# An adaLN block with guided-trajectory attention and two windowed-attention layers: setup as steps, roots by a seed and small operations, unit multiply per tile, padded stream, folded norm, Gelu steps together

## The reference

```python
mod = silu(c) @ wmod                        # sa, ca, ga, sb, cb, gb; ga, gb kept at 0.25 or more in size
h = layernorm(x) * (1 + ca) + sa
x = x + ga * guided_trajectories(h)         # normed steps, dots with 64 guides, softmax, weighted sum
y = layernorm(x) * (1 + cb) + sb
for l in range(2):
    h = shift_token(y)                      # features 64..127 come from the row before, zero in front
    q, k, v = split(h @ wqkv[l])            # 8 heads of 64
    q, k = rotary(l2norm(q) * qs, l2norm(k) * ks)
    y = y + local_attention(q, k, v) @ wo[l]          # windows of 64 rows, each sees the one before
    h = (shift_token(y) - mu) / sqrt(var + 1e-5) * ln_g[l] + ln_b[l]
    a, g = split(h @ w1[l] + b1[l])         # 341 columns each
    y = y + (a * gelu(g)) @ w2[l] + b2[l]
x = x + gb * y
```

## Time and profile before

| what | value |
| --- | --- |
| three runs, median (lowest to highest) | 967.34 us (966.5 to 968.35) |
| the profiled execution | 966.96 us, of which 965.0 is its span |
| mean granted TensorE clock | 0.942 |
| PE / DVE / ACT / POOL busy | 786.4 / 668.0 / 659.3 / 539.6 us |
| ACT's table loads | 40, each 1.283 us |
| power of 128x32 on POOL | 32 times, 5438 ns each |
| DVE's unit multiply 128x2048 | 32 times, 2534 ns each |
| DVE's L1393, bank by rotary table | 128 times, 684 ns each |

### The profile page before, as it was taken

The page is one execution under the profiler, slowest core; times in us unless marked ns, Lnnn a source line. Parts: engine busy times, 40 slices in busy tenths (PEclk is TensorE's granted clock), DMA queues, the critical chain, the costliest instruction groups (busy, mean ns, idle before and its releaser), DMA issues.

```text
span 965.0 us, 19306 instructions
## 1 busy us (share of the span) xinstructions
PE 786.4 (81%) x7151; PEld 556.3 (58%) x7151; DVE 668.0 (69%) x1588; ACT 659.3 (68%) x1545; POOL 539.6 (56%) x324
## 2 busy tenths in 40 slices
PE   4456788879889989888969979888888989888874
PEld 4334566656556666655657656656565666656543
DVE  4566876685687877586887967486787776676732
ACT  0234766867576985877786886877675887868672
POOL 2046853493956653394985643293966690576600
PEclk9668789999899999999999999999999999999997
DMA  6000000000000000000000000000000000000000
GB/s 206 0 12 1 12 2 1 1 1 2 1 2 1 23 2 22 2 1 1 1 1 2 23 1 23 1 2 1 1 1 2 12 2 13 2 1 2 1 1 22
DMA packets 12275, 9.85 MB, mean 10 GB/s; under 512 B 1040, under 2 KB 11288, under 8 KB 12184
## 3 DMA queue, kind: packets, MB, share of 16 engines
q1 hardware_dynamic: 12184, 8.64, 3.0%
HBM read 6.54 MB, written 2.10 MB: 9 GB/s over the span
## 4 chain that ended last, share of the span: by engine, by line
PE 40%; DVE 20%; ACT 19%; issue 11%; POOL 9%; DMA 0%; SPq 0%; POOLq 0%; ACTq 0%; DVEq 0%
ACT probs L964 7%; PE pair L696 6%; PE mixed L727 5%; POOL qk L1494 4%; PE dense L831 4%; PE pair L759 3%; DVE space L1393 3%; DVE q_norm L1398 3%; PE dense L795 3%; PE dense L796 2%; PE dense L797 2%; DVE qk L1195 2%; PE dense L908 2%; ACT squares L1083 2%; ACT probs_t L972 2%
## 5 line engine op out<-in xcount | busy, mean ns | idle before, releaser
L1494 POOL TENSOR_TENSOR qk<-space 128x512 f32<-128x512 f32 x128 | 186.4, 1463 | 58.0 <-DVE q_norm L1398 55.1
L1454 POOL TENSOR_TENSOR root<-power,minus_half 128x32 f32<-128x32 f32 x32 | 174.0, 5438 | 4.6 <-DVE power L1404 4.6
L964 ACT ACTIVATE probs<-pair,neg_max 128x128 f32<-128x128 f32 x512 | 138.3, 402 | 18.9 <-DVE neg_max L1215 18.5
L1393 DVE TENSOR_TENSOR space<-dense,tables 128x512 f32<-128x512 f32 x128 | 87.5, 684 | 36.9 <-ACT space L1087 35.2
L908 PE MATMUL dense<-wq_hi,h_hi 128*128 128x512 f32 x192 | 90.2, 470 | 26.6 <-DVE space L1393 10.9
L1491 POOL TENSOR_TENSOR space<-space,tables 128x512 f32<-128x512 f32 x64 | 82.7, 1293 | 50.7 <-ACT space L1087 50.7
L696 PE MATMUL pair<-eye_s,probs 128*128 128x128 f32 x512 | 80.9, 292 | 34.9 <-ACT probs L964 34.7
L1215 DVE TENSOR_REDUCE neg_max<-pair 128x4 f32<-128x512 f32 x128 | 82.0, 684 | 35.2 <-PE pair L759 35.1
L1083 ACT ACTIVATE squares<-dense 128x512 f32<-128x512 f32 x128 | 79.1, 618 | 39.5 <-PE dense L910 38.6
L696 PEld LDWEIGHTS pair<-eye_s,probs 128*128 128x128 f32 x512 | 59.1, 146 | 56.2 <-ACT probs L964 51.9
L1398 DVE TENSOR_REDUCE q_norm<-squares 128x8 f32<-128x512 f32 x128 | 86.4, 675 | 0.0
(11 more groups left out here) (166 smaller groups left out, 1809.2 us busy)
## 6 DMA issues: line engine op xcount, KB each, us to landing
x_in<-n_L_attn_embeddings_dram SPq DMA_DIRECT2D x8, 256.0 KB, 3.0
out_dram<-hn SPq DMA_DIRECT2D x8, 256.0 KB, 2.4
qk<-in_L_ffn_wqkv_dram SPq DMA_DIRECT2D x1, 1536.0 KB, 6.2
qk<-in_L_ffn_w_dram SPq DMA_DIRECT2D x1, 682.0 KB, 7.5
wo_s<-in_L_ffn_wo_dram SPq DMA_DIRECT2D x2, 256.0 KB
o_t<-in_L_wmod_dram SPq DMA_DIRECT2D x1, 384.0 KB, 3.3
probs<-const_rotary_dram SPq DMA_DIRECT2D x1, 256.0 KB, 3.6
band_s<-const_band_dram SPq DMA_DIRECT2D x1, 256.0 KB, 7.8
```

Of the source, the lines that this page charges most:

```text
L964: last = act.activation(probs[:, ring, hh, :], banks[m][:, hh * P:(hh + 1) * P], ACT.Exp, bias=neg_max[:, ring, hh:hh + 1], scale=1.0)
L1393: dve.tensor_tensor(turned_s[:, t % 2, m, :].rearrange("p (h a b) -> p h a b", h=HEADS, a=2), halves[:, :, ::-1, :], rot(layer, t, 2 * m + 1),
L1454: return pool.tensor_tensor(to, of, minus_half[:, 0:of.shape[-1]], ALU.pow)
L1494: pool.tensor_tensor(qk[s][:, t, m * INNER:(m + 1) * INNER], turned_c[:, t % 2, m, :], turned_s[:, t % 2, m, :], ALU.add).then_inc(added, 1)
```

## The change

The setup's pieces become steps (`setup.silu`, `setup.gate`, ...) in the tables. PE begins after the load of the unit matrix alone. ACT makes the high part of wqkv. The inverse root of the guides is one power on POOL instead of Newton steps on DVE.

The roots of q and k: DVE makes a halved sum and an integer seed (`proj.root`), POOL refines it by ten small operations, each waiting for the one ahead. The unit multiply is per tile, 128x1024 (64 of them). POOL's add waits until DVE has read the bank, no longer for the sum of the squares.

The streams have a zero column in front (`SEQ + 1`), so that a projection reads shifted tokens directly: DVE rounds two half-partition pieces (`proj.hi`), and the low part is taken by POOL for partitions 0 to 63 and by DVE for 64 to 127 (`proj.lo`). The feed-forward's `stats` still shifts on ACT.

ln_g is multiplied into w1 once, and ln_b @ w1 is added to b1 once (12 matmuls with one column, `setup.bias`). The feed-forward's norm then copies the bank to `h_hi` on ACT, and DVE subtracts from the same bank for `h_lo` (`ff.lo`). The half rows of v which the next window needs are copied by SP's DMAs (`cross_values`, 64) instead of ACT (L1092).

Attention's turn, flip and mix have one step for each m, and the up chunks one for each half. All four tables are written anew. Two lines of PE's first table:

```diff
-        3:new.turn 3:new.dots 3:new.mix 3:new.sum 3:new.stream"""),
+        3:setup.silu 3:setup.rows 3:setup.mod 3:setup.guide 3:new.turn 3:setup.gate 3:new.dots 3:setup.bias
+        3:new.mix 3:new.sum 3:new.stream"""),
```

The exps stood between the Gelu steps; now they stand behind them. In the code, the projection and the roots:

```diff
-        y_new = [sb(f"y_new{s}", [P, 2, SEQ]) for s in range(2)]
-        y_t = [sb(f"y_t{s}", [P, 2, SEQ]) for s in range(2)]
+        y_new = [sb(f"y_new{s}", [P, 2, SEQ + 1]) for s in range(2)]
+        y_t = [sb(f"y_t{s}", [P, 2, SEQ + 1]) for s in range(2)]
...
+        def shifted_halves(stream_):
+            return ((slice(0, P // 2), stream_[0:P // 2, :, 1:SEQ + 1]), (slice(P // 2, P), stream_[P // 2:P, :, 0:SEQ]))
...
             # DVE, projections
-                elif what == "split":
-                    wait_halves_free(dve, i, slot, PROJ)
-                    dve.wait_ge(qkv_shifted, before + 1)
-                    dve.tensor_copy(h_hi[:, :], flat(shifted)).then_inc(qkv_hi, 1)
+                elif what == "hi":
+                    wait_split_free(dve, i, slot, PROJ)
...
+                    dve.wait_ge(*written(i, slot))
+                    for rows, view in shifted_halves(proj_source(i, slot)):
+                        last = dve.tensor_copy(by_seq(h_hi[rows, :]), view)
+                    last.then_inc(qkv_hi, 1)
+                elif what == "lo":
+                    dve.wait_ge(qkv_hi, before + 1)
+                    rows, view = shifted_halves(proj_source(i, slot))[1]
+                    dve.tensor_tensor(by_seq(h_lo[rows, :]), view, by_seq(h_hi[rows, :].bitcast(F32)),
+                                      ALU.subtract).then_inc(qkv_lo_high, 1)
...
-                elif what == "rsqrt":
-                    pair_ = 2 * before + step[2]
-                    dve.wait_ge(summed, 4 * pair_ + 4)
-                    dve.tensor_scalar(power[:, :], q_norm[:, :], 1e-24, None, ALU.max).then_inc(qk_powered, 1)
+                elif what == "root":
...
+                    dve.tensor_scalar(half[:, :], q_norm[:, :], 1e-24, 0.5, ALU.max, ALU.mult).then_inc(seed_self, 1)
+                    dve.wait_ge(seed_self, pair_ + 1)
+                    dve.tensor_scalar(root[:, 0, :].bitcast(I32), half[:, :].bitcast(I32), -0.5, RSQRT_SEED, ALU.mult,
+                                      ALU.add).then_inc(qk_seeded, 1)
                 elif what == "unit":
-                    unit_length(s, before, step[2])
+                    t = step[2]
+                    dve.wait_ge(added, 2 * (4 * before + t) + 2)
+                    dve.wait_ge(qk_rooted, 2 * before + t // 2 + 1)
+                    rows = qk[s][:, t, :].rearrange("p (h d) -> p h d", d=DH)
+                    dve.tensor_tensor(rows, rows, root[:, 0, 16 * (t % 2):16 * (t % 2) + 16].rearrange("p (h o) -> p h o", o=1)
+                                      .broadcast_to([P, 2 * HEADS, DH]), ALU.mult).then_inc(qk_ready, 1)
             # POOL
-                inverse_root(root[:, :], power[:, :]).then_inc(qk_rooted, 1)
+                pool.tensor_tensor(z, y, half[:, :], ALU.mult).then_inc(qk_newton, 1)
+                pool.wait_ge(qk_newton, count)
+                for k in range(3):
+                    pool.tensor_tensor(scratch[:, :], y, z, ALU.mult).then_inc(qk_newton, 1)
+                    pool.wait_ge(qk_newton, count + 1)
+                    pool.tensor_tensor(scratch[:, :], threes[:, :], scratch[:, :], ALU.subtract).then_inc(qk_newton, 1)
+                    pool.wait_ge(qk_newton, count + 2)
+                    if k < 2:
+                        pool.tensor_tensor(to[:, :, :], to[:, :, :], scratch[:, :].rearrange("p (o h) -> p o h", o=1)
+                                           .broadcast_to([P, 2, 32]), ALU.mult).then_inc(qk_newton, 1)
...
+                        pool.tensor_tensor(y, y, scratch[:, :], ALU.mult).then_inc(qk_rooted, 1)
```

The norm of the feed-forward, its fold in the setup, and v's half rows:

```diff
             # ACT, feed-forward norm
-                    act.activation(hn[:, :], src[:, :], ACT.Identity, scale=columns[:, ROW_LN_G + layer:ROW_LN_G + layer + 1],
-                                   bias=columns[:, ROW_LN_B + layer:ROW_LN_B + layer + 1]).then_inc(empty(i, slot, step), 1)
+                    act.activation(h_hi[:, :], bank(i, slot, step)[:, :], ACT.Copy).then_inc(ff_hi, 1)
             # DVE, feed-forward
-                elif what == "hi":
...
-                    dve.tensor_copy(h_hi[:, :], hn[:, :]).then_inc(ff_hi, 1)
+                elif what == "lo":
+                    dve.wait_ge(ff_hi, before + 1)
+                    src = bank(i, slot, (FF, "norm"))
+                    dve.tensor_tensor(h_lo[:, :], src[:, :], h_hi[:, :].bitcast(F32),
+                                      ALU.subtract).then_inc(empty(i, slot, (FF, "norm")), 1)
             # DVE, setup
+                    last = dve.tensor_tensor(bias, bias, pair[0][0][:, 0:6 * DEPTH], ALU.add)
+                    for layer in range(DEPTH):
+                        last = dve.tensor_scalar(stage_1[:, layer, :], stage_1[:, layer, :],
+                                                 columns[:, ROW_LN_G + layer:ROW_LN_G + layer + 1], None, ALU.mult)
             # ACT, projections
-                        act.activation(v_cross[s][half_rows, t // 2, :, 0:DH], heads[half_rows], ACT.Copy)
             # SP
+                        sp.wait_ge(*read_at(i, slot, (PROJ, "tile", t, 2)))
+                        rows = slice(WIN * half_, WIN * half_ + WIN)
+                        sp.dma_start(v_cross[s][rows, p, :, :], v[s][rows, t, :, :]).then_inc(v_crossed[s][p], 16)
             # PE, attention mix
+                    if t % 2:
+                        pe.wait_ge(v_crossed[s][t // 2], 32 * (before // 2 + 1))
```

More of the change, by code:

```diff
@@ L238 @@
         steps("""
-        3:new.stats 3:new.turn 3:new.dots 3:new.sims 3:new.weights 3:new.gate 3:new.again 3:new.stream"""),
+        3:new.stats 3:setup.square 3:setup.silu 3:setup.columns 3:setup.mod 3:setup.wide 3:setup.guide
+        3:new.turn 3:setup.dots 3:setup.lo.0 3:setup.lo.1 3:setup.gate 3:new.dots 3:new.sims 3:new.weights
+        3:setup.ff 3:new.gate 3:new.again 3:new.stream"""),
         steps("""
-        2:new.stats 2:proj.keep 2:new.turn 2:proj.split 2:proj.tile.0.0 2:proj.tile.0.1 2:proj.tile.1.0
@@ new lines @@
+        2:proj.root.0 2:proj.tile.2.0 2:proj.norm.2.0 2:proj.norm.2.1 2:proj.tile.2.1 2:proj.tile.3.0
+        2:proj.unit.0 2:proj.unit.1 2:proj.norm.3.0 2:proj.tile.3.1 2:proj.norm.3.1 2:proj.root.1 2:new.dots
+        3:a.score.0.0 3:a.score.0.1 2:proj.unit.2 2:proj.unit.3 2:new.sims 3:a.mix.0.0 3:a.mix.0.1
+        3:a.score.1.0 3:a.score.1.1 2:new.weights 3:a.mix.1.0 2:new.gate 2:new.again 3:a.mix.1.1
+        3:a.score.2.0 3:a.score.2.1 2:new.stream 3:new.stats 3:proj.keep 3:a.mix.2.0 3:proj.hi 3:new.turn
@@ new lines @@
+        3:a.mix.2.1 3:proj.tile.1.1 3:proj.norm.1.1 3:a.mix.3.0 3:a.mix.3.1 3:proj.root.0 3:proj.tile.2.0
+        3:proj.norm.2.0 3:proj.tile.2.1 3:proj.unit.0 3:a.project 3:proj.norm.2.1 3:proj.unit.1
+        3:proj.tile.3.0 3:proj.norm.3.0 3:proj.tile.3.1 3:proj.norm.3.1 3:proj.root.1 3:ff.lo >0:a.score.0.0
+        3:ff.up.0 >0:a.score.0.1 3:proj.unit.2 3:proj.unit.3 3:ff.up.1 3:ff.up.2 >0:a.score.1.0
+        >0:a.score.1.1 3:ff.down 3:new.dots 3:new.sims 3:store.turn"""),
+        steps("""
@@ new lines @@
+        2:proj.tile.3.1 2:proj.norm.3.1 2:proj.root.1 2:ff.lo 3:a.score.0.0 2:new.gate 2:proj.unit.2
+        2:proj.unit.3 2:ff.up.0 2:new.again 2:ff.up.1 3:a.score.0.1 2:ff.up.2 2:new.stream 3:a.score.1.0
+        2:ff.down 3:a.score.1.1 2:store.turn 3:proj.hi 3:a.mix.0.0 3:a.mix.0.1 2:proj.keep 3:proj.lo
+        3:ff.stats 3:a.mix.1.0 3:a.mix.1.1 3:proj.tile.0.0 3:proj.norm.0.0 3:ff.norm 3:proj.tile.0.1
+        3:a.score.2.0 3:a.score.2.1 3:proj.norm.0.1 3:a.score.3.0 3:a.score.3.1 3:proj.tile.1.0
@@ L789, in attention @@
+                    last.then_inc(mixed_full, 1)
                 elif what == "out":
```

1328 lines of the change are left out of this document (778 added, 550 removed).

## The result

The changed kernel takes 985.15 us (median of 4, 983.77 to 987.5), the kernel before 966.92 beside it: 1.0189 times as long, with an interval of 1.0166 to 1.0212. The forecast was 917, and the range ended at 950.

A forecast was written before the change was run, and what follows sets the result against it. TensorE's matmuls (786.4 of 965.0 us busy) were taken as a floor, its 178.6 idle us as winnable. Terms -2 - 9 - 33 - 3 - 1.5 = -48.5 took 966.96 to 918.5, rounded to 917; range 880 to 950 (8 in 10).

The forecast's parts named there:

- The chain's price: POOL's roots of q and k: ten chained small operations at 0.32 us, 3.2 per root instead of 5.44.
- POOL's h_lo out of PE's waits: Middle stages: DVE subtracts from PSUM instead of POOL, winning back 5 of PE's 6.8 us of waits.
- two table loads in the last stage: ACT around the last stage's Gelus: two loads instead of six, of which PE sees 3 us.
- three signs of being wrong: PE's idle time outside setup not falling some 45 us, a root over 5.4, or DVE rows of waits above 30.
- start and first stages together: Setup to first regular stages: -2 us for the first projection's start, 9 of 20.0 idle us taken back.
- the part on contention: POOL held beside DVE's two-input multiplies: per-tile ones hold twice for half as long, same sum; up to 38 us of POOL.
- L1404's 0.33: DVE's root steps: the seed adds a second small operation priced at 0.33 us, 32 of them, 10.6 in all.
- the 29 of the forecast: DVE's busy time over the whole kernel: +29 us, to 697.
- 48.5 us off PE's idle time: Whole kernel: the sum of start, middle and end terms, -2 - 9 - 33 - 3 - 1.5.
- the middle's 33: Regular stages: 33 of 101.8 idle us won from PE's waits for h_lo, o_t, probs_t, k_t, exp and space.
- R2: Rival: DVE, the one engine gaining work, is the next limit; L1393's waits double, time 947 us; chance 0.12.
- R3: Rival: POOL's chain is slower than the power, 10.1 us per root instead of 5.44, time 993; chance 0.07.

The follow-up runs named there:

- e2: The changed kernel with the unit multiply per two tiles again (128x2048) instead of per tile; 990.17 us.
- e8: The changed kernel with each unit multiply replaced by a one-input sum over the same elements, the multiplication left out; 964.77 us.
- e12: The changed kernel with one DVE operation per root step and the unit multiplies replaced by sums (multiplication left out); 960.07 us.
- e4: The changed kernel with one DVE operation per root step and the unit multiply per pair of tiles; 984.63 us.
- e7: The changed kernel with the half rows of v copied by ACT again instead of by DMAs; 993.64 us.
- e16: The kernel before, in its old order, with chain, one seed operation, DMA copies, padded streams and split unit multiply; 959.38 us.
- e1: The changed kernel with one DVE operation less per root step: ACT's scaled squares give the halved sum, the seed is taken from it directly; 978.58 us.
- e15: The kernel before, in its old order, with chain, one seed operation, DMA copies and padded streams, multiply per pair; 944.55 us.
- e5: The changed kernel with two more DVE sums of a constant 128x512 tile, read by nobody, between the two operations of each root step; 1004.08 us.
- e3: The changed kernel with the one power of 128x32 on POOL back in place of seed and ten-operation chain; 1053.18 us.

## Why the prediction was wrong

**Right.** The chain's price (3.4 us, 3.2 said), POOL 438 (444) and ACT 601 (596), POOL's h_lo out of PE's waits, two table loads in the last stage. Of the three signs of being wrong only the first came: PE's idle time didn't fall by 45 us. A root takes under 5.4 us, and no single DVE row of PE's waits is above 30. POOL's part of the projection's low, beside DVE's, took 1.24 us in one group of eight and 1.56 in the other, so longer than 1.27 in half of the cases. The first projection starts at 56.45, 5.2 us earlier, where 2 were said; start and first stages together won 8.8 us of idle time up to the first residual, where 11 were said. Behind the last residual 0.9 us were won of 1.5. What the four spared table loads of the last stage gave (3 were said) can't be seen, as the stretch from the twelfth residual to the sixteenth became 25.8 us longer.

**Two steps failed**, of 68 us between 917 and 985. The first is in the part on contention: "Per-tile multiplies hold it twice for half as long, so the sum is the same", with a price for POOL alone and none for DVE. The trace of after shows no sharing in proportion to length: a held DVE instruction waits for the end of POOL's instruction in flight, and its cost goes by the number of meetings (0.42 us per instruction of 1024, 0.36 per one of 2048 in e2). 32 multiplies became 64, and the small root operations, which I priced at L1404's 0.33, pay it as well. Behind the earlier trace rows stood instructions of 0.165 to 1.25 us, which the mean of 0.33 hid. Of DVE's +70 us, 44 are held time; the other 26 are near the 29 of the forecast. In time the multiply's holding costs 20.4 us (e8), and 25.1 together with one root operation (e12). The split isn't the mistake by itself: in the new order it wins 5 or 6 us (e2, e4).

The second step is the rest, 43 us: e12, whose held time of 17 us is near the 14 of before, takes 960.07. The forecast took 48.5 us off PE's idle time and called PE's busy time unchanged, "775 to 787". In e12 the idle time is only 15.4 us under before (178.6 to 163.2), and the busy time 8.1 above it (794.5). So the sum of idle time won back, of which the middle's 33 is the largest term, was three times too large, and the new order makes PE's own work longer, which the forecast put at nothing.

**The middle's sum of 33** was argued from each wait by itself. Between the first and the sixteenth residual, those for exp, probs_t, k_t and o_t fell from 56.7 to 45.9 us, by 11 where 21 were expected; e7's 0.25 us per microsecond of ACT fits that. Those for L1393's successor rose from 18.2 to 23.4 instead of falling by 7. Those for the multiply rose from 2.2 to 23.3. Those for POOL's h_lo fell from 7.1 to 0.4 and those for o_t from 5.4 to 2.7, near what was said.

**The order.** I took the new tables as a gain or as neutral. Together with fold and setup they cost 19 us with the split multiply and 40 without it, in spite of the better start. Two things are seen in that. PE is longer busy, by 21 and 28 us. And roots and multiplies stand in the path of PE's next turn: its waits for the multiply are 10.4 us in e16 and 27.5 in e1. Which of the tables' moves does either, and what fold and setup have in it, wasn't separated, so the cause of this larger part stays open.

**The rivals.** R2 named the engine (697 against a measured 738) but not the mechanism. R3 named the right sign for a wrong reason: no operation of the chain costs over 0.33 us.

**The account**, from before to after: chain, one seed operation and DMA copies -23; split multiply and padded streams +15.5; new order, fold and setup +19; the second root operation +6.6. That is +18, as it must be, since each term is the difference of two neighbouring runs. By the other way, over e15 and e4, it is -23; +0.7 for the streams; +40 for new order, fold and setup; -6 for the split; +6.6. The terms hold only in their order.

## What to carry to other kernels

Before moving work between DVE and POOL, look at the shortest and longest time of each DVE instruction that reads and writes SBUF: if they differ by one POOL instruction, count meetings, not lengths, and keep small ones away from POOL's bursts. Test the parts of a large change in the old order first: here chain and DMA copies bring 1.3%, with the seed in one operation 2.3%, and the whole costs 1.9%. And don't look at waits alone: compare PE's busy time as well, since a new order can make the same matmuls take longer. An experiment that adds work to an engine shows what a microsecond costs at that place (0.25 for ACT's copies, 0.47 for sums on DVE in the root's path), not what the engine's load costs everywhere.

## What the runs showed of the hardware

A DVE multiply of two SBUF inputs (1.21 us for 128x1024) and POOL's two-input adds (1.27) did not run side by side (4.59 us for two of each). POOL is held as well: with the multiplies replaced, its adds fell from 1.405 to 1.28 us. A `tensor_scalar` of 128x32 from SBUF to SBUF, one input, was held too (0.17 alone, 0.74 on average), with int32 and with a stride of two on its output as well; `tensor_reduce` from SBUF wasn't held: all 64 took 1.202 to 1.222 us for 1024 columns (e8), and 0.668 to 0.680 for 512 (e5). With the power back (e3) PE was idle 220 us instead of 188, its mean granted clock was 0.906 instead of 0.950, and its busy time was 34 us longer for the same matmuls. The Trainium skill ("GPSIMD Engine Reference", Key points) names two SBUF inputs or a two-port mode as what contends; the small operations agree if they run in that mode, which no run shows. By the Trainium skill ("VectorE: DVE Perf Modes", the section on the TRN2 errata) the split costs 0.16 us per pair, an estimate from the page; the undisturbed instructions agree, 2 x 1.226 - 2.293 = 0.16 by the medians, and the 15.5 us that the split cost in the old order are another thing.
